# New tables for the order of work in layers 0, 1 and 3 of a four-layer kernel

## The reference, cut to what matters

```
layer 0: multi-query attention (16 heads of 8) followed by a Mamba block
         (a convolution of 4 taps, a selective scan over 256 channels x 16 states), + 32 experts with a gate
layer 1: attention (16 heads of 64) + a feed-forward of width 352 with FP4 quantised operands
layer 2: attention (16 heads of 8) + a switch with 8 experts of limited capacity
layer 3: a selective scan over 128 channels x 16 states with a layer norm, + 8 routed and 2 shared experts of width 64
```

## Time and profile before

| | us |
|---|---|
| median of 3 runs (3024.81 to 3029.01) | 3028.58 |
| the profiled execution | 3028.86 |
| its span | 3027.5 |
| TensorE matmul busy | 2419.8 (80%) |
| VectorE busy | 2214.6 (73%) |
| ScalarE busy | 1437.6 (47%) |
| GpSimd busy | 868.9 (29%) |

### The profile page before, as it was taken

How to read it: one execution, slowest core, us unless ns; L and a number is a source line. 1 busy time by engine, 2 the same in 40 slices (tenths; PEclk the granted TensorE clock), 3 DMA queues, 4 the chain that set the end, 5 groups by cost and what they waited for, 6 DMA issues and landing times. The chain is left out here.

```text
span 3027.5 us, 47754 instructions
## 1 busy us (share of the span) xinstructions
PE 2419.8 (80%) x18201; PEld 1712.4 (57%) x18201; DVE 2214.6 (73%) x4587; ACT 1437.6 (47%) x3688; POOL 868.9 (29%) x453
## 2 busy tenths in 40 slices
PE   4788888888888675798888989867999986766766
PEld 2456555555566464466666666644666654544544
DVE  3488888888887844578787777754666634999998
ACT  0344545444544511466666676632334434555453
POOL 0033344434344420123232232310000001454543
PEclk9989999999999887799999999987999998888888
DMA  1011011101110154000000000000000002444443
GB/s 61 15 36 36 29 43 36 36 29 36 37 43 29 50 165 151 1 1 2 1 1 1 1 1 1 1 34 14 28 28 14 7 19 92 145 163 139 164 154 109
DMA packets 71348, 147.97 MB, mean 49 GB/s; under 512 B 6864, under 2 KB 37072, under 8 KB 70608
## 3 DMA queue, kind: packets, MB, share of 16 engines
q1 hardware_dynamic: 69072, 140.73, 13.8%
q0 software_dynamic: 2048, 4.20, 0.4%
HBM read 135.20 MB, written 9.18 MB: 48 GB/s over the span
## 5 line engine op out<-in xcount | busy, mean ns | idle before, releaser
L2091 POOL TENSOR_TENSOR h<-h,Crep 128x1024 f32<-128x1024 f32 x128 | 383.3, 3005 | 705.7 <-DVE h L1514 705.7
L2073 POOL TENSOR_TENSOR pr<-pr,rsum 128x512 f32<-128x512 f32 x192 | 227.5, 1188 | 617.6 <-DVE rsum L1358 617.6
L1392 DVE TENSOR_REDUCE mx<-psum 128x4 f32<-128x1024 f32 (+1 forms) x192 | 229.0, 1217 | 116.4 <-PE psum L656 116.4
L1514 DVE TENSOR_TENSOR_SCAN h<-dA,h 128x1024 f32<-128x1024 f32 x128 | 291.9, 2295 | 2.4 <-ACT dA L1977 1.8
L831 PE MATMUL psum<-h,pack_wf 128*128 128x256 f32 x1024 | 257.5, 409 | 5.4 <-POOL h L2091 5.4
L2125 POOL TENSOR_TENSOR h<-h,Crep 128x1024 f32<-128x1024 f32 x64 | 184.8, 2888 | 253.9 <-DVE h L1268 253.9
L831 PEld LDWEIGHTS psum<-h,pack_wf 128*128 128x128 f32 x1024 | 209.2, 209 | 43.0 <-POOL h L2091 6.4
L1880 ACT ACTIVATE pt<-psum 128x1024 f32<-128x1024 f32 x192 | 187.5, 1022 | 96.7 <-PE psum L658 96.7
L1836 ACT ACTIVATE pr<-psum,nb 128x256 f32<-128x256 f32 (+1 forms) x512 | 210.8, 429 | 46.5 <-DVE nb L1350 43.7
L1977 ACT ACTIVATE dA<-delta,A 128x255 f32<-128x255 f32 x512 | 210.2, 495 | 12.2 <-DVE h L1514 10.8
L1505 DVE TENSOR_TENSOR h<-dtu,psum 128x512 f32<-128x512 f32 x256 | 164.2, 676 | 69.1 <-PE psum L818 61.5
(11 more groups left out here) (342 smaller groups left out, 5446.1 us busy)
## 6 DMA issues: line engine op xcount, KB each, us to landing
Crep<-c_rows SPq DMA_DIRECT2D x64, 512.0 KB, 3.8
Brep<-bc_rows SPq DMA_DIRECT2D x64, 512.0 KB, 6.5
Crep<-bc_rows SPq DMA_DIRECT2D x64, 512.0 KB, 7.0
w1r<-m_w SPq DMA_DIRECT2D x32, 256.0 KB, 5.8
w2r<-m_w SPq DMA_DIRECT2D x32, 256.0 KB, 5.6
pack_wf<-wf SPq DMA_DIRECT2D x1, 3192.0 KB, 13.3
slots<-zero SPq DMA_DIRECT2D x12, 256.0 KB, 3.0
w1s<-s_w SPq DMA_DIRECT2D x8, 256.0 KB, 2.7
```

The costliest lines, as they stand in the source:

```text
L1392: ve.e.tensor_reduce(mx[:, qb, 2 * h:2 * h + 2, groups[0]:groups[-1] + 1], k.psum[:, base:base + 2, :].rearrange("p i (n x) -> p i n x", n ...
L1514: ve.e.tensor_tensor_scan(flat(h), flat(k.dA[c][g % 2]), flat(h), 0.0, ALU.mult, ALU.add).then_inc(*k.set("scanned", 0, b, g, c))
L2073: po.e.tensor_tensor(p3, p3, bcast(k.rsum[n][:, 0:len(heads[r])], P * (q + 1), 2), ALU.mult).then_inc(*k.set("normed", 1, b, p, r))
L2091: po.e.tensor_tensor(h[:, :, :], h[:, :, :], k.Crep[n % 3][:, :, :], ALU.mult).then_inc(*k.set("hC", 0, b, g, c))
```

## The change

Only the numbers in `ORDER[0]`, `ORDER[1]` and `ORDER[3]` change. The same steps are issued with the same instructions, the same buffers, waits and DMAs; layer 2 and the experts are as they were. Of the diff the tables of layer 0 and the rows of the others in which the order changes most:

```
-        "pe_out": (3, 7, 10, 12, 14, 17),
-        "pe_results": (0, 16),
-        "pe_states": (1, 11, 13, 23, 25, 30, 35, 41, 44),
-        "pe_summing": (2, 8, 19, 28, 34),
+        "pe_out": (3, 7, 8, 12, 13, 17),
+        "pe_results": (0, 14),
+        "pe_states": (1, 11, 19, 21, 23, 31, 34, 42, 44),
+        "pe_summing": (2, 9, 16, 28, 36),
...
-        "ve_inner": (4, 32, 39, 42, 43, 44, 45, 48, 49, 51, 53, 55),
-        "ve_states": (1, 2, 7, 10, 14, 22, 24, 26, 28, 38, 40, 41, 46, 52, 57, 58, 60),
-        "ve_wide0": (5, 11, 15, 27, 29, 47, 50),
+        "ve_inner": (3, 31, 34, 39, 40, 41, 42, 43, 47, 48, 54, 55),
+        "ve_states": (1, 9, 10, 11, 22, 23, 24, 26, 29, 30, 37, 38, 46, 49, 56, 58, 60),
+        "ve_wide0": (4, 15, 16, 25, 28, 51, 52),
...
-        "ve_ffn": (6, 7, 8, 9, 10, 11, 12, 13, 14, 15, 16, 17, 18, 25, 27, 28, 31, 33, ...
+        "ve_ffn": (4, 5, 6, 8, 9, 10, 11, 12, 13, 14, 15, 17, 18, 25, 27, 28, 31, 32, ...
...
-        "ve_states3": (1, 8, 9, 14, 23, 26, 27, 31, 46),
-        "ac_states3": (1, 10, 11, 12, 29),
+        "ve_states3": (1, 7, 14, 15, 16, 28, 29, 35, 36),
+        "ac_states3": (1, 6, 13, 14, 26),
```

More of the change, by code:

```diff
@@ L228 @@
     0: {
-        "pe_inner": (4, 20, 22, 29, 33),
-        "pe_out": (3, 7, 10, 12, 14, 17),
-        "pe_pre0": (6, 21, 24, 27, 36, 38, 40, 43),
-        "pe_results": (0, 16),
-        "pe_states": (1, 11, 13, 23, 25, 30, 35, 41, 44),
-        "pe_summing": (2, 8, 19, 28, 34),
-        "pe_wide0": (5, 9, 15, 18, 26, 31, 32, 37, 39, 42),
-        "ve_inner": (4, 32, 39, 42, 43, 44, 45, 48, 49, 51, 53, 55),
-        "ve_out": (3, 8, 9, 12, 13, 18, 19),
-        "ve_pre0": (6, 17, 20, 23, 30, 31, 33, 34, 35, 36, 37, 54, 56, 59, 61),
@@ L239 @@
-        "ve_results": (0, 16, 21, 25),
-        "ve_states": (1, 2, 7, 10, 14, 22, 24, 26, 28, 38, 40, 41, 46, 52, 57, 58, 60),
-        "ve_wide0": (5, 11, 15, 27, 29, 47, 50),
[L242 to L246, removed]
-    },
-    1: {
[L249 to L262, removed]
@@ new lines @@
+        "pe_inner": (4, 20, 22, 29, 32),
+        "pe_out": (3, 7, 8, 12, 13, 17),
+        "pe_pre0": (6, 24, 26, 27, 35, 38, 41, 43),
+        "pe_results": (0, 14),
+        "pe_states": (1, 11, 19, 21, 23, 31, 34, 42, 44),
+        "pe_summing": (2, 9, 16, 28, 36),
+        "pe_wide0": (5, 10, 15, 18, 25, 30, 33, 37, 39, 40),
+        "ve_inner": (3, 31, 34, 39, 40, 41, 42, 43, 47, 48, 54, 55),
+        "ve_out": (2, 7, 8, 12, 13, 19, 20),
+        "ve_pre0": (5, 6, 17, 21, 32, 33, 35, 36, 44, 45, 50, 53, 57, 59, 61),
@@ new lines @@
+        "ve_results": (0, 14, 18, 27),
+        "ve_states": (1, 9, 10, 11, 22, 23, 24, 26, 29, 30, 37, 38, 46, 49, 56, 58, 60),
+        "ve_wide0": (4, 15, 16, 25, 28, 51, 52),
+        "ac_inner": (2, 15, 16, 17, 19, 20, 28, 29, 30),
+        "ac_out": (1, 5, 13),
+        "ac_pre0": (4, 7, 8, 18, 21, 22),
+        "ac_states": (0, 6, 9, 10, 14, 26, 27, 34, 35),
+        "ac_wide0": (3, 11, 12, 23, 24, 25, 31, 32, 33, 36),
+    },
+    1: {
+        "pe_attend": (0, 4, 6, 7, 10, 11, 12, 13, 14, 20, 21, 22, 27, 28, 29, 30, 33, 35, 36, 37, 38, 39, 42, 43, 44, 45),
+        "pe_ffn": (1, 16, 17, 18, 23, 25, 47, 48, 49, 51),
+        "pe_pre1": (2, 5, 8, 9, 15, 19, 24, 26, 31, 32, 41, 46, 50, 52),
+        "pe_spread1": (3, 34, 40),
+        "ve_attend": (0, 3, 7, 16, 19, 20, 21, 22, 23, 24, 26, 29, 30, 34, 40, 41, 42, 46, 47, 48, 49, 53, 57, 59, 63, 64, 69),
+        "ve_ffn": (4, 5, 6, 8, 9, 10, 11, 12, 13, 14, 15, 17, 18, 25, 27, 28, 31, 32, 33, 35, 36, 37, 38, 39, 43, 44, 45, 51,
+            52, 60, 61, 68),
+        "ve_pre1": (1, 58, 62, 65, 67),
+        "ve_spread1": (2, 50, 54, 55, 56, 66),
+        "ac_attend": (0, 6, 7, 9, 10, 12, 13, 14, 15, 17, 23, 24, 29, 30, 31, 34, 36, 37, 38, 39, 41, 42, 43, 44, 45, 46, 47,
+            48, 49, 55, 56),
+        "ac_ffn": (1, 3, 16, 19, 20, 21, 25, 27, 28, 32, 50, 51, 52),
+        "ac_pre1": (2, 4, 8, 11, 18, 22, 26, 33, 35, 40),
+        "ac_spread1": (5, 53, 54),
```

## The result

| | before | after |
|---|---|---|
| median of 4 runs each, us | 3028.26 (3024.81 to 3029.01) | 2913.98 (2913.45 to 2917.5) |
| ratio, with its 95% interval | | 0.9626 (0.9614 to 0.9637) |
| the profiled execution, us | 3028.86 | 2917.5 |
| its span, us | 3027.5 | 2916.2 |
| a full turn of layer 0, us | 61.4 | 53.3 |

A forecast was written before the change was run, and what follows sets the result against it. Layer 0 was taken as bound by its order (neither VectorE nor TensorE full), layer 1 by TensorE; layer 3's VectorE was busy 27.7 of 29.26 us. Layers 0, 1, 3: 3028.86 - 76 - 6 + 3 = 2950 us, range 2922 to 2990.

The forecast's parts named there:

- the ends: Layer 0, about four turns with fewer blocks in flight: half a full turn's saving each, 11 us in all.
- added for the slower clock: Layer 0's turn: the stretches gave 55.5 us, raised by a half to 56.0.
- 0.7 because `sum3` would take 4.67 us: Layer 0, first stretch: `sum3` 0.7 us late for `prod1,0` at 4.67, covered by two scans if it takes 3.6.
- The 0.3 for `max1`: Layer 0, first stretch: `max1` ends 0.3 us behind `scan1,1`, as `y_out` ahead of `keys0` waits for `yT`.
- a wait of 1.9 at `gz`: Layer 0, second stretch: `gate` behind `keys1`, estimated at over 3 us, makes VectorE wait 1.9 us.
- 17.0 and 2.7: Layer 0, second stretch, TensorE: 17.0 us from `w_in0` to the end of `bc`, 2.7 more to `spr(3,1)`.
- rival (b): Layer 0: TensorE's clock slows in the new order; a turn of 65 us, 3080 in all, chance 0.06.
- `xn`'s 2.0 us: Layer 0, first stretch: `xn` moves to where GpSimd is idle, so its 2.0 us of waiting go.
- -6 forecast: Layer 1: a turn ends 0.8 us earlier at best, taken as 0.4; 15 turns, 6 us saved.
- +3 forecast: Layer 3: new waits outweigh those saved by 0.2 us a turn; 15 turns, 3 us lost.
- (a): Layer 0: only GpSimd's share goes, VectorE still waits for TensorE; 3.4 us a turn saved, 2981, chance 0.22.
- (c): Layers 1 and 3 give back 1 us a turn each, by `hq0` and the router's tail; 2983, chance 0.10.

The follow-up runs named there:

- e7: Kernel before, with 13 more matmuls of no use per turn of layer 0, in three TensorE waits: ratio 0.9965, turn 60.37 us.
- e14: Changed kernel without the 5 matmuls of no use ahead of `y_out`: ratio 0.9708, turn of layer 0 55.52 us.
- e6: Kernel before, with `xn` moved ahead of `scan1,0`, where GpSimd is idle: ratio 0.9999, turn of layer 0 61.49 us.
- e5: Changed kernel, with `xn` put back behind `scan1,0`, beside GpSimd's multiplication: ratio 0.9663, turn of layer 0 54.21 us.
- e10: Kernel before, with layer 0's new tables for TensorE and VectorE, ScalarE's old: ratio 0.9936, turn of layer 0 59.16 us.
- e9: Kernel before, with layer 0's new table for TensorE alone: ratio 1.0621, turn of layer 0 75.08 us.
- e2: Kernel before, with the new tables of layer 1 alone: ratio 0.9998, median 3027.8 us.
- e3: Kernel before, with the new tables of layer 3 alone: ratio 0.9984, median 3024.5 us.
- e11: Changed kernel, with `delta` and `dtu` put back right behind `scan3,0`, beside GpSimd's multiplication: ratio 0.9878, turn of layer 0 58.75 us.

## Why the prediction was wrong in size

**Right.** What the change does in layer 0 was right in direction and place: the waits for `spr(2,1)` and `max2` went, `xn` and `dtu` are short, no wait at `mx` is over 1 us. 12 turns by 8.1 are 97 of the 108.6 us, and 11.5 are left for the ends. The forecast had 11 there, but that fits by luck: its rule, half a turn's saving in four turns, gives 16 with the 8.1 that a turn did save. Of the 32.6 us by which layer 0 saved more than the 76 forecast, all are the turn's: 53.3 instead of 56.0.

**The mis-sized term** is the turn of layer 0, in the durations that I carried over. By my three cuts, in the turn shown above:

| stretch | forecast | measured |
|---|---|---|
| `kTv` to the end of `scan1,1` | 20.0 | 18.95 (474.69 to 493.64) |
| to `prod3,1` | 20.2 | 19.1 (to 512.77) |
| to the next `kTv` | 15.3 | 15.2 (to 528.00) |
| added for the slower clock | 0.5 | 0 |

In the first I charged 0.7 because `sum3` would take 4.67 us as in the earlier trace rows; it takes 3.62, the alternative that I had named, and nothing is late. The 0.3 for `max1` was booked in the wrong stretch: the wait at `mx` lies behind `scan1,1` and is 0.62 (493.64 to 494.27), more than forecast. In the second stretch TensorE takes 15.7 from `w_in0` to the end of `bc` (494.29 to 510.00) instead of 17.0. I took `keys1` at over 3 us from its first part of 1.72, and so a wait of 1.9 at `gz`; `keys1` takes 2.2 and the wait is 0.64. The two terms that the prediction gives for this stretch, 17.0 and 2.7, add up to 19.7; 0.5 of its 20.2, for what lies between `scan1,1` and `w_in0`, is not written out (measured 0.65).

Both slow durations, 4.67 and 1.72, came from stretches with a granted clock of 0.62 and 0.78. I had seen that those clocks follow TensorE's waits, and that the new order removes these waits, and still kept the slow durations and put a half on top. The three terms, 0.7, 1.3 (15.7 instead of 17.0) and the half, are 2.5 of the 2.7 us. No run puts the slow durations back at these two places, so their share is read off the trace of the changed kernel; what the runs show is the size of such a term: more matmuls in the old order's waits bring back 1.0 us a turn (e7), and one slow place in the new order costs 1.6 in the usual turn (e14). The Trainium skill (page TensorE: Matmul & The Clock Gate, section What's actually happening) has the throttled state as the default, which activity lifts; the rows agree (`keys0` takes 1.15 us with the five matmuls of no use and 2.09 without). I had used it for a loss only, as rival (b), where it spoke as much for a gain.

**Right for a wrong reason.** I booked `xn`'s 2.0 us as saved by its move. In the old order that move saves nothing (e6), in the new one being early is worth 0.9 (e5): a lock's price is that of the path at that time, not its duration. The sum of the first stretch was right all the same, since I cut the turn on VectorE; that an earlier end of it might only lengthen a wait in the second was not asked.

**Not seen.** The prediction calls VectorE's idle time nearly all waits for TensorE. One of 1.33 us a turn, longer than the 0.93 that it lists, is for ScalarE:

```profile
496.41 0.15 DVE L1036 RECIPROCAL gs<-gs 32x1 f32<-32x1 f32 x1 [1.33 <-ACT gp L1706]
```

In the new order `u` stands ahead of this step and it waits no more; `u` waits 0.66 for ScalarE instead. I also gave ScalarE's moves no worth of their own, for ScalarE is busy 28.9 of 61.4 us. Without them the change is worth 2.2 of its 8.1 us a turn (e10). The sum did not suffer, since it was made for all tables together. Nor did I expect the partial kernels to be slower than before (e9).

**Layers 1 and 3.** Layer 1: -6 forecast (bounds in us a turn -1.5 to +1), nothing measured (e2). The two waits for the copy between `qk` steps did fall, from 1.9 to 1.3 us a turn. Over ten turns of the kernel before another of these copies cost

```profile
PE psum L389 <- ACT qT L1739: 9.3, 10, 0.9
```

and over ten of the changed one the waits are

```profile
PE psum L389 <- ACT kT L1739: 12.7, 20, 0.9
PE psum L389 <- ACT qT L1739: 12.0, 10, 1.2
...
PE psum L925 <- DVE hq L1614: 4.5, 10, 0.5
...
PE psum L925 <- ACT hqT L2049: 2.6, 10, 0.3
```

That other wait grew by 0.3 a turn, and the matmuls of `hq0` wait 0.7, within my "up to 0.8", where they had no wait before. Together these take back more than the 0.6 gained. The 0.4 that I booked was half of the best case, chosen without a row.

Layer 3: +3 forecast, -4.6 measured (e3), and by the windows of the two profiles a turn is 0.2 us shorter (29.26 to 29.04) where I had it 0.2 longer. The subtraction in `maxidx,sub` takes 1.22 us instead of 0.80 on average (0.15 to 1.02 in twelve turns of the kernel before), so it costs 0.4, more than my 0.3. What I overrated are the waits at `hs1,0` (0.27 instead of 0.4) and for `g2exp` (0.18 instead of 0.3) and the meeting of `zmx` with GpSimd (0.27 instead of 0.4); `hs3,1` is longer by 0.01 instead of 0.1, and a wait of `x_ssm` of 0.17 on average, which I had not listed, is gone. Rivals (a), (b) and (c) did not occur.

## What to carry to other kernels

In this kernel durations of matmuls read beside a low granted clock (`sum3` 4.67 at 0.62) belonged to the old order; where a new order removes the idle times ahead of them, put in the duration of the same shape at full clock (3.62), and keep the slow one for the bound. An order that fits several engines is one thing: count it for all tables together, and expect part of it alone, one engine's or without the one that is "only" half busy, to be worth little or to lose. Time that an instruction spends locked out by another engine is worth what the path loses there: of the same 2.0 us nothing in one order (e6) and about half in the other (e5). Where a third engine waits behind it, the loss can be larger than the lock: 5.4 us a turn behind a lock of 1.9 and 1.4 of moved work (e11).
